# Moving small work to other key tiles in a fused attention and expert kernel

## What is computed

```python
x = x + tanh(g_xattn[0]) * attention(layernorm(x), ctx, ctx)   # scores, softmax over 1601 keys, values, Wo + bo
n = layernorm(x)
scores = softmax(n @ router_w + router_b)
G, idx = top_k(scores.T, 512)
h1 = relu(n[idx] @ w1 + b1)
eo = h1 @ w2 + b2
x = x + tanh(g_ffn[0]) * scatter_add(eo * G)
```

## Time and profile before

| | us |
|---|---|
| median of 3 runs (591.82 to 592.48) | 592.31 |
| the profiled execution | 591.86 |
| its span, first to last instruction | 590.1 |
| PE busy | 549.7 (93%) |
| DVE busy | 446.4 (76%) |
| ACT busy | 391.0 (66%) |
| POOL busy | 214.4 (36%) |
| mean granted clock of PE | 0.992 |

### The profile page before, as it was taken

How to read it: one execution, slowest core, us unless ns; L and a number is a source line. 1 busy time by engine, 2 the same in 40 slices (tenths; PEclk the granted TensorE clock), 3 DMA queues, 4 the chain that set the end, 5 groups by cost and what they waited for, 6 DMA issues and landing times.

```text
span 590.1 us, 12821 instructions
## 1 busy us (share of the span) xinstructions
PE 549.7 (93%) x5043; PEld 318.8 (54%) x5043; DVE 446.4 (76%) x811; ACT 391.0 (66%) x762; POOL 214.4 (36%) x205
## 2 busy tenths in 40 slices
PE   7798899999999999999998988899999999999994
PEld 4433333334343333433333344479889898898973
DVE  3889879996999969899896268656767868676541
ACT  2587778987789878898887830054665656555651
POOL 3058075001925018200167010240644626446234
PEclk9999999999999999999999999999999999999998
DMA  8600000001000000100000105012735656355133
GB/s 280 244 2 1 1 1 3 2 1 38 2 37 2 2 37 1 38 1 2 37 37 2 38 18 163 18 55 81 167 110 108 153 134 144 107 109 160 19 37 36
DMA packets 23808, 35.80 MB, mean 61 GB/s; under 512 B 3460, under 2 KB 16197, under 8 KB 23621
## 3 DMA queue, kind: packets, MB, share of 16 engines
q1 hardware_dynamic: 17604, 26.59, 13.9%
q0 software_dynamic: 6144, 8.39, 8.1%
HBM read 26.59 MB, written 8.39 MB: 59 GB/s over the span
## 4 chain that ended last, share of the span: by engine, by line
PE 72%; DVE 17%; issue 4%; ACT 3%; POOL 1%; DMA 1%; POOLq 0%; DVEq 0%; ACTq 0%; SPq 0%
PE ps L1728 15%; PE ps L1735 15%; PE ps L1497 14%; DVE mquart L1025 9%; PE ps L1463 7%; PE ps L1484 7%; PE ps L1393 2%; PE ps L1354 2%; ACT probs L752 2%; PE ps L1369 1%; PE ps L1706 1%; PE ps L1681 1%; DVE mparts L1041 1%; PE ps L1506 1%; ACT osb L651 1%
## 5 line engine op out<-in xcount | busy, mean ns | idle before, releaser
L1025 DVE TENSOR_REDUCE mquart<-ps 128x2 f32<-128x802 f32 x256 | 240.6, 986 | 28.4 <-PE ps L1463 25.9
L752 ACT ACTIVATE probs<-ps 128x512 f32<-128x512 f32 (+1 forms) x416 | 223.6, 596 | 27.0 <-PE ps L1484 22.6
L1497 PE MATMUL ps<-probs,vp 128*32 128x256 f32 (+1 forms) x1664 | 133.5, 393 | 4.2 <-ACT osb L651 4.1
L1463 PE MATMUL ps<-kpad,qrows 64*128 64x401 bf16 x512 | 89.6, 337 | 5.9 <-DVE mquart L1025 5.0
L1484 PE MATMUL ps<-qfull,kpad 64*128 64x256 bf16 (+1 forms) x832 | 86.8, 273 | 1.1 <-ACT x L773 0.9
L1322 DVE TENSOR_TENSOR h1l<-hf,h1h 128x512 fp32r<-128x512 f32 x64 | 44.3, 692 | 55.8 <-ACT hf L877 45.9
L876 ACT ACTIVATE h1h<-ps,b1T 128x512 fp32r<-128x512 f32 x64 | 43.9, 687 | 54.3 <-PE ps L1728 52.5
L1735 PE MATMUL ps<-w2h,h1h 128*128 128x256 f32 x256 | 73.8, 288 | 2.2 <-DVE h1l L1322 1.5
L1735 PE MATMUL ps<-w2l,h1h 128*128 128x256 f32 x256 | 72.4, 283 | 0.0
L1735 PE MATMUL ps<-w2h,h1l 128*128 128x256 f32 x256 | 72.3, 282 | 0.0
L621 POOL DMA_INDIRECT out<-eo,idx_put x32 | 55.4, 1732 | 26.1 <-ACT eo L886 16.9
(11 more groups left out here) (200 smaller groups left out, 732.5 us busy)
## 6 DMA issues: line engine op xcount, KB each, us to landing
w1raw<-in_L_ffn_w SPq DMA_DIRECT2D x16, 512.0 KB, 4.7
w2raw<-in_L_ffn_w SPq DMA_DIRECT2D x16, 512.0 KB
xs<-in_x SPq DMA_DIRECT2D x4, 512.0 KB, 7.8
ctx_sb<-in_ctx SPq DMA_DIRECT2D x3, 512.0 KB, 6.0
out<-xs SPq DMA_DIRECT2D x3, 512.0 KB, 4.3
x_rows<-x SPq DMA_DIRECT2D x3, 512.0 KB, 2.6
b2b<-in_L_ffn_b SPq DMA_DIRECT2D x1, 1024.0 KB, 11.6
out<-xs SPq DMA_DIRECT2D x2, 256.0 KB, 2.0
```

The source lines that it names most:

```text
L752: nc.scalar.activation(out_p, ps[0:w, next_bank(), :], ACT.Exp, scale=float(SCALE)).then_inc(s_ex, 1)
L1025: nc.vector.tensor_reduce(mquart[:, u % 2, t, a, :, kq], ps[:, b:b + 2, 0:MAXW], AX.X, ALU.max).then_inc(s_mr, 1)
L1463: last = mm(ps[:, bank + b, 0:MAXW], qrows[band(b), g, q:q + P], kpad[band(b), g, a, lo:lo + MAXW], start=True, stop=True)
L1497: last = mm(ps[32 * hh:32 * hh + 32, PV, 0:UW], vp[0:w, kt, g, hh, :], probs[0:w, step % PROBS, hh, :], start=(kt == 0), stop=(kt == NKT - 1))
```

## The change

The tables get other numbers, and POOL's list gets one wait. The lines that carry it:

```diff
-        PLACE = 10
+        PLACE = 11
-        O_THIS, O_LAST, BACK_AT, WO_AT = (2, 4), (0, 4), (0, 7), (0, 12)
-        XN_AT, Q_AT = ((0, 9), (0, 11)), ((1, 3), (1, 6))
-        X2_AT, ROUTER_AT = ((2, 6), (2, 7)), ((2, 9), (2, 12))
+        O_THIS, O_LAST, BACK_AT, WO_AT = (2, 5), (0, 5), (0, 7), (0, 9)
+        XN_FIRST, XN_LATER, Q_AT = ((0, 7), (0, 9)), ((0, 0), (0, 3)), ((1, 3), (1, 7))
+        X2_AT, ROUTER_AT = ((2, 7), (2, 9)), ((2, 10), (3, 0))
...
-        LN1_AT = {(u, NKT - CT + t): (c, t) for c, u in ((2, 1), (3, PER_CHUNK + 1)) for t in range(CT)}
-        LN2_AT = ((1, 4), (1, 5), (1, 6), (1, 7))
+        LN1_AT = {(u, kt): (c, ts) for c, u in ((2, 1), (3, PER_CHUNK + 1)) for kt, ts in ((7, (0, 1)), (8, (2, 3)))}
+        LN1_DONE = {(1, 9): 2, (PER_CHUNK + 1, 9): 3}
+        LN2_AT = {3: (0, 1), 4: (2, 3)}
+
+        def xn_at(c):
+
+            return XN_FIRST if c == 0 else XN_LATER
...
                 for pair in range(PAIRS):
                     a, f = 2 * P * pair, 2 * pair
+                    if pair == PAIRS // 2:
+                        pool.wait_ge(s_mp, UNITS)
                     pool.wait_ge(s_w1in[pair // 2], 16)
...
-                    if c > 0 and (r, kt) in LN2_AT:
-                        ln2_stats(c - 1, LN2_AT.index((r, kt)))
-                    if c > 0 and (r, kt - 1) == LN2_AT[-1]:
+                    if c > 0 and r == 1:
+                        for t in LN2_AT.get(kt, ()):
+                            ln2_stats(c - 1, t)
+                    if c > 0 and (r, kt) == (1, 5):
                         ln2_aggr(c - 1)
```

More of the change, by code:

```diff
@@ L363, in part_tiles, with values_at, take_at @@
             return range(CT) if c < LAST else range(UQ * half, UQ * half + UQ)
-        LN1_AT = {(u, NKT - CT + t): (c, t) for c, u in ((2, 1), (3, PER_CHUNK + 1)) for t in range(CT)}
-        LN2_AT = ((1, 4), (1, 5), (1, 6), (1, 7))
+        LN1_AT = {(u, kt): (c, ts) for c, u in ((2, 1), (3, PER_CHUNK + 1)) for kt, ts in ((7, (0, 1)), (8, (2, 3)))}
[3 more added lines that the diff above has]
+            return XN_FIRST if c == 0 else XN_LATER
+        def values_at(u, kt):
+            return [(u, kt - 2) if kt > 1 else (u - 1, NKT - 2 + kt)] if u > 0 or kt > 1 else []
+        def take_at(u):
+            return 1
         FIRST_VALUES, FIRST_KEYS, FIRST_QUERIES = (2, 6, 10, 13), (3, 7), 11
@@ L813, in _ @@
                     exp(u, kt, 1)
-                    if kt == 1 and u > 0:
+                    if kt == take_at(u) and u > 0:
                         take_o(u - 1)
@@ L822, in _ @@
                             scale_wo(c - 1, odd, next_bank())
-                    if c + 1 < NC and (r, kt) in XN_AT:
-                        take_xn(c + 1, XN_AT.index((r, kt)), next_bank())
+                    if c + 1 < NC and (r, kt) in xn_at(c):
+                        take_xn(c + 1, xn_at(c).index((r, kt)), next_bank())
                     if c + 1 < NC and (r, kt) in Q_AT:
@@ L1121, in _ @@
                         normalise(c - 1, 1, 0, next_bank())
-                    if c > 0 and (r, kt) in LN2_AT:
-                        ln2_stats(c - 1, LN2_AT.index((r, kt)))
-                    if c > 0 and (r, kt - 1) == LN2_AT[-1]:
+                    if c > 0 and r == 1:
+                        for t in LN2_AT.get(kt, ()):
+                            ln2_stats(c - 1, t)
+                    if c > 0 and (r, kt) == (1, 5):
                         ln2_aggr(c - 1)
                     if (u, kt) in LN1_AT:
-                        ln1_stats(*LN1_AT[u, kt])
-                    if kt == 0 and (u - 1, NKT - 1) in LN1_AT:
-                        ln1_aggr(LN1_AT[u - 1, NKT - 1][0])
+                        to, ts = LN1_AT[u, kt]
+                        for t in ts:
+                            ln1_stats(to, t)
+                    if (u, kt) in LN1_DONE:
+                        ln1_aggr(LN1_DONE[u, kt])
                     if (u, kt) == (UNITS - 1, 0):
@@ L1602, in _ @@
                         max_tile(n)
[L1603 to L1606, removed]
+                    for step in values_at(u, kt):
+                        pv(*step)
                     if kt == PLACE and u + 1 < UNITS:
@@ L1618, in _ @@
                         wo(c - 1, range(CT), (even, next_act((s_wt, 2 * c))))
-                    if c + 1 < NC and (r, kt) in XN_AT:
-                        k = XN_AT.index((r, kt))
+                    if c + 1 < NC and (r, kt) in xn_at(c):
+                        k = xn_at(c).index((r, kt))
                         transpose_xn(c + 1, k, next_act((s_Tt, KD * (c + 1) + k + 1)))
```

## The result

| | before | after |
|---|---|---|
| median of 4 runs, us | 592.37 (591.82 to 592.48) | 588.08 (587.38 to 588.88) |
| ratio, with its 95% interval | | 0.993 [0.9913, 0.9947] |
| the profiled execution, us | 591.86 | 587.38 |
| its span, us | 590.1 | 585.6 |
| DVE busy, us | 446.4 | 442.3 |

The change makes the kernel 4.3 us faster, where 4.8 us slower was forecast. The time is that of rival (a), 587.8. Nearly all of the span's 4.5 us lies in the attention: from ACT's first take of queries to its last take of the output (L666 now) it is 4.4 us shorter (290.27 against 294.65). It starts 0.2 us sooner, and what comes after takes 248.0 us before and 248.1 after.

What follows compares the result with a forecast made beforehand. PE, DVE and ACT were taken to be full together in units without side work. Wait -3.1, side work -2.3 and second norm's statistics +10.2 sum to +4.8 us: 597.1 us in the median, range 587.0 to 600.5.

Steps and rivals of the forecast that it cites:

- rival (a): Unit 13: the join waits for at most one of L539's four instructions, 0.9 us; 587.8 us; chance 0.28 with both cases.
- The wait half way: Unit 14: the second half of POOL's first weights waits for the last join, so nothing holds it; -3.1 us.
- Side work of units 0 to 12: Statistics behind query projections, moved rows and output projection, and later placing fill PE's idle time; -2.3 us together.
- Placing one tile later gives 0.3 in all: Within the side-work term: PE waited at placing for the join in unit 5, so later placing gains 0.3 us.
- which loosens a cluster: 0.2 each of PE's 0.9 us: Units 4, 8 and 12: turned rows and output projection move to earlier key tiles, gaining 0.2 us each.
- DVE's dry spells in unit 5 could be filled: Unit 5: two statistics behind each query projection fill 0.7 us of each gap, 1.98 and 0.70 us; gain taken 0.6.
- The second norm's statistics: Unit 13: statistics closed earlier make POOL's L539 and weights run over the join of unit 14's maxima; +10.2 us.
- If it is held as in unit 14, to the pause: Unit 13: the join offered inside L539 waits until POOL pauses, ending at 309.35 instead of 299.95; 9.4 us.
- a hold of one instruction could be told from the long one at 5.4 us: Rival (a) decides once the hold in unit 13 is under 5.4 us, the sum of the two gains.
- four instructions in unit 14 without giving way: Against rival (a): unit 14's join was held through L558, L560, L562 and L565, POOL passing on four times.
- unit 13 near 17 us: Sign for rival (a): unit 13 stays near 17 us and its join takes at most 1.4 us.
- no unit from 1 to 12 longer: Sign for the side-work term: none of these units lengthens, and units 1 and 5 shorten by 0.5 us each.

Runs made afterwards that it cites:

- twelve spare ones: Kernel before plus the new wait half way, with 12 unused POOL scalings run over the join of unit 13; 589.23 us, ratio 0.9944.
- the small program: A kernel of its own: POOL chains of one instruction kind each, beside 44 DVE joins or 24 casts; 44 joins took 4.36 us beside scalings, 3.48 alone.
- the weights in that place: Changed kernel, with POOL's first two weight pairs ahead of the second norm of chunk 2 instead of after it; 587.88 us, ratio 0.9922.
- the last version above: Changed kernel, with turned rows, output projection and output turn of chunks 1 to 3 back at their old places; 588.05 us, ratio 0.9927.

## Why the prediction was wrong, step by step

**The wait half way: right in mechanism, too small.** Forecast -3.1 with bounds of 2.6 and 3.5, measured -3.8 (588.59 against 592.37), 3.6 in the windows. Its sign, its place and its witnesses came as written: last join 0.2 us, third pair just after it, no PE standing for it, no slow clock. The size was off because unit 10 (18.11) was too long a measure for unit 14: without the hold unit 14 takes 17.55 us. I had also given the term to the wait alone. The changed kernel loses the stall without it too, and pauses of under 0.1 us do the same.

**Side work of units 0 to 12: mis-sized.** Forecast -2.3, bounds -4.7 to +0.5. The changed kernel against the one with the wait alone gives -0.5 in the medians (588.08 against 588.59, ranges that overlap) and -0.8 in the attention of the two traces (290.27 against 291.06 us), with what the statistics change in units 13 and 14 in it. By windows of the units, before against after: units 0, 1, 5, 6 and 10 gain 0.70, 0.36, 0.22, 0.31 and 0.16, together 1.75. Units 3 with 4, 7 with 8, and 11 with 12 lose 0.35, 0.34 and 0.33, unit 9 0.11: -0.6 in the units up to 12. (Unit 13 then loses 0.17, and unit 14 goes from 17.55 to 17.21.) Two steps failed.

The first is "Placing one tile later gives 0.3 in all". A unit whose work is the same has the same window to 0.02 us in all traces of these kernels, so the last version above can be held against the other two, unit by unit (us):

| unit | before | changed | old places back, PLACE at 11 |
|---|---|---|---|
| 3 | 15.37 | 16.44 | 15.71 |
| 4 | 19.79 | 19.07 | 19.48 |
| 11 | 15.38 | 15.69 | 15.69 |
| 12 | 18.45 | 18.47 | 18.68 |

The window of unit 3 in that version, columns as above:

```profile
107.31:123.02 15.71, 15.26 (x197) 5.57 (x191) 15.24 (x20) 14.47 (x30) 0.00 (x0) 1.00 0.01 3
```

Of the tables, only PLACE is other than before in the window of unit 3, and it is 0.34 us longer; units 7 and 11 are 0.32 and 0.31 longer. So in a unit without side work placing one tile later costs 0.3 us where it was to gain. This is read off the tables; no run moved PLACE alone, and why it costs is open.

The second is "which loosens a cluster: 0.2 each of PE's 0.9 us". Unit 12 has no rows to turn, and there the new places of the output projection gain 0.21 us (18.68 to 18.47). But in units 4 and 8 the rows are turned as well, and the first of the two turns, at key tile 0, falls into the window of the full unit ahead (15.37 us, PE busy 15.06): against the version with the old places back, unit 3 grows by 0.73 while unit 4 shrinks by 0.41. That DVE's dry spells in unit 5 could be filled was right; there they are 1.33 and 0.70 us now, against 1.98 and 0.70:

```profile
146.15 1.89 DVE L1040 TENSOR_REDUCE mquart<-ps 128x2 f32<-128x802 f32 x2 [1.33 <-PE ps L1481]
...
153.01 1.89 DVE L1040 TENSOR_REDUCE mquart<-ps 128x2 f32<-128x802 f32 x2 [0.70 <-PE ps L1481]
```

**The second norm's statistics: the step that decided, and wrong.** Forecast +10.2, measured nothing. The schedule was right to within 1.2 us: L965 closed at 294.6 where I had 295.65, L539 from 296.27 where I had 297.3, the join offered at 298.55 where I had 299.75, inside it. The step that failed here, and that turned the forecast the wrong way, is "If it is held as in unit 14, to the pause". It took one long hold, behind casts and subtractions late in a chain, for a property of POOL as such. Two things were wrong in that. First, L539 is another kind of instruction: its scalings, with one SBUF tensor as input, let the joins pass (0.19 us in this kernel and beside twelve spare ones; 44 joins beside four of them in the small program, none over 0.37 us). Second, even casts and subtractions hold a join for about one instruction early in a chain (0.37 us with the weights in that place), so 9.4 us would not have come about there either.

The Trainium skill, "SBUF — State Buffer", section "SBUF: two separate sides", has the shared pair held "for the whole instruction". The early holds here agree with it, 1.23 us beside subtractions of 1.26 to 1.27. The scalings don't: they read SBUF and held a join for 0.2 of their 1.23 us. Nor do the late holds, which ran over seven casts in a row.

**The rivals.** The time is rival (a)'s, and the bound it was weighed by was right: a hold of one instruction could be told from the long one at 5.4 us. But (a) too expected up to 1.2 us of hold in unit 13, and its reason, that POOL gives way between L539's four, was not needed. In the changed kernel itself the join happens to fall at the change from the second scaling to the third and so fits that reason too; it is the join 0.45 us into a spare scaling, and the 44 of the small program, that rule it out. That the sum came out to 0.3 us is luck: a term too large (side work) and one too small (the wait) nearly cancel. The evidence that I set against it, four instructions in unit 14 without giving way, was correct and is a case of its own. The witness for (a), unit 13 near 17 us, was there; the one for the second term, "no unit from 1 to 12 longer", was not.

## What to carry to other kernels

Where a tiny DVE operation with two SBUF inputs sits on the critical path, ask what kind of instruction POOL runs beside it and how long its chain has run unbroken. In these runs scalings of one tensor cost it at most 0.2 to 0.5 us, casts and subtractions about the length of one of them, and a long chain with casts in it the rest of the chain; short pauses in such a chain, such as a wait of POOL for its own last result behind every fourth instruction, were as good as a rearrangement. Before one stall is used to price another, check that the instruction, its kind and its place in the queue are the same; and when work is moved out of a crowded unit, price the unit that it moves into.

## What the runs showed of the hardware that was not expected

- POOL's tensor-with-scalars instructions and DVE's join of two SBUF inputs run nearly side by side: 44 joins take 4.36 us beside four scalings of 128x256 and 3.48 alone, one join in each scaling being longer by 0.2 us (by 0.4 to 0.5 with scalings of 128x512). Memsets let them pass undisturbed (26 in 1.92 us).
- DVE's casts of SBUF data, one input only, are also held beside casts and subtractions: 6 run in the 4.96 us of four subtractions. Beside four scalings both sides slow down a little: 24 casts take 4.28 us and alone 3.34, and the scalings 1.35 us each instead of 1.23 (5.41 against 4.92 for four).
- Late in an unbroken chain with casts, the hold goes on to the chain's end, over up to 8.86 us. It follows from none of these: what stands behind the join, POOL's semaphore waits, the phase of the start, an earlier join, or the chain's length in microseconds alone (subtractions 13.1 us in: 0.37 us). **What turns the short hold into the long one stays open.** A plain count of POOL's instructions does not fit either: 17 casts had ended at the earliest long hold seen with casts alone and 14 instructions of the mix, but only 6 where four of them were scalings, while after 10 subtractions the hold was still short.
